# Splitting the row gathers of a graph-attention kernel into five turns behind VectorE's phases

## The reference

```
h     = max(layernorm(x), 0)
xl    = h @ hetero_w[node_type] + hetero_b[node_type]
eae   = lrelu(edge_attr @ edge_attr_w);  ete = lrelu(edge_type_emb[edge_type])
alpha = lrelu(concat(xl[dst], xl[src], ete, eae) @ att_w)
alpha = softmax of alpha over the edges that share a dst
msg   = concat(xl[src], eae) @ lin_w * alpha
out   = x + segment_sum(msg, dst)
```

## Time and profile before

| | |
|---|---|
| median of 3 runs | 5781.72 us (5751.97 to 5784.94) |
| profiled execution | 5821.55 us, its span 5819.7 us |
| PE busy | 3413.9 us, 59% of the span |
| POOL busy | 2783.2 us, 48% |
| DVE busy | 2540.0 us, 44% |
| ACT busy | 878.1 us, 15% |
| mean granted TensorE clock | 0.762 |
| DMA moved | 284.25 MB, mean 49 GB/s |

### The profile page before, as it was taken

How to read it: one execution, slowest core, us unless ns; L and a number is a source line. 1 busy time by engine, 2 the same in 40 slices (tenths; PEclk the granted TensorE clock), 3 DMA queues, 4 the chain that set the end, 5 groups by cost and what they waited for, 6 DMA issues and landing times.

```text
span 5819.7 us, 64841 instructions
## 1 busy us (share of the span) xinstructions
PE 3413.9 (59%) x21563; PEld 1921.9 (33%) x21563; DVE 2540.0 (44%) x6672; ACT 878.1 (15%) x2080; POOL 2783.2 (48%) x2793
## 2 busy tenths in 40 slices
PE   3456565665665565555666565666665666665660
PEld 2233333333333333333333333333333333333340
DVE  6343443443443444344444444444444444443464
ACT  2011111111111111111111111111111111111120
POOL 2554454454454444444554445455454454444417
PEclk7677777777787787777777777787777777777785
DMA  6111121121121121111211211211211211211112
GB/s 187 26 44 42 42 54 43 42 53 42 42 53 42 42 50 44 42 42 42 54 42 46 48 42 43 51 44 42 53 42 42 53 42 42 53 42 42 47 36 72
DMA packets 187871, 284.25 MB, mean 49 GB/s; under 512 B 74956, under 2 KB 142782, under 8 KB 186752
## 3 DMA queue, kind: packets, MB, share of 16 engines
q1 hardware_dynamic: 72864, 159.20, 9.5%
q0 software_dynamic: 90368, 55.56, 7.7%
q10 hardware_dynamic: 24288, 64.79, 3.1%
HBM read 207.03 MB, written 72.29 MB: 48 GB/s over the span
## 4 chain that ended last, share of the span: by engine, by line
another core or an unknown queue 37%; PE 29%; issue 17%; DVE 15%; POOL 2%; DMA 1%; DVEq 0%; SPq 0%; ACT 0%; POOLq 0%; ACTq 0%
PE ps_misc L678 21%; PE ps_pick L690 6%; DVE dst_f L1021 3%; DVE dscore L1055 2%; DVE sums L1148 2%; DVE gath L1048 1%; DVE node_buf L1083 1%; DVE h L1042 1%; POOL hib L515 1%; DVE onehot L1068 1%; PE ps_msg L722 1%; PE ps_attr L699 0%; DVE node_buf L1102 0%; PE ps_misc L645 0%
## 5 line engine op out<-in xcount | busy, mean ns | idle before, releaser
L481 POOL DMA_INDIRECT gath<-table_dram,meta x2675 | 2672.8, 999 | 2877.0 <-DMA meta<-meta_in 2003.3
L678 PE MATMUL ps_misc<-parts,dst_f 128*128 128x462 bf16 x9450 | 2345.3, 405 | 694.4 <-issue 615.4
L678 PEld LDWEIGHTS ps_misc<-parts,dst_f 128*128 128x128 bf16 x9450 | 988.7, 107 | 1921.5 <-issue 1187.0
L690 PE MATMUL ps_pick<-s_dst,onehot 122*128 122x128 bf16 x9375 | 736.5, 232 | 1402.7 <-DVE dscore L1055 895.8
L1055 DVE TENSOR_REDUCE dscore<-ps_pick 128x4 f32<-128x512 f32 x875 | 538.0, 629 | 1660.9 <-remote 1462.5
L690 PEld LDWEIGHTS ps_pick<-s_dst,onehot 122*128 122x128 bf16 x9375 | 609.2, 104 | 1559.0 <-DVE dscore L1055 948.5
L1042 DVE TENSOR_TENSOR h<-ps_misc,sel_mask 128x462 f32<-128x462 f32 x450 | 285.7, 635 | 1384.2 <-remote 1020.6
L575 ACT ACTIVATE wts<-args 128x50 f32<-128x50 f32 x125 | 30.7, 246 | 3484.4 <-DVE args L1126 2719.8
L588 ACT COPY rows<-sums 128x825 f32<-128x825 f32 x125 | 223.5, 1788 | 1080.6 <-DVE sums L1148 1080.6
L1021 DVE TENSOR_SCALAR dst_f<-dst_f,part_group 128x128 bf16<-128x128 f16 x1750 | 355.7, 284 | 0.9 <-DMA dst_f<-sel_code_dram 0.9
L1048 DVE TENSOR_REDUCE gath<-h 128x33 f32<-128x462 f32 x450 | 281.3, 625 | 2.7
(11 more groups left out here) (230 smaller groups left out, 1215.1 us busy)
## 6 DMA issues: line engine op xcount, KB each, us to landing
hib<-digit_dram SPq DMA_DIRECT2D x125, 612.5 KB
rows_dram<-rows ACTq DMA_DIRECT2D x125, 437.5 KB
gath<-table_dram,meta POOLq DMA_INDIRECT x2675
attr<-edge_attr_t_in SPq DMA_DIRECT2D x125, 200.0 KB
dst_f<-sel_code_dram SPq DMA_DIRECT2D x125, 128.0 KB
hib<-digit_dram SPq DMA_DIRECT2D x250, 50.0 KB
rows_dram<-gath ACTq DMA_DIRECT2D x1, 8575.0 KB, 46.8
hib<-digit_dram SPq DMA_DIRECT2D x250, 25.0 KB
```

The source lines that it names most:

```text
L481: nc.gpsimd.indirect_dma_start(gath[u][:, t, :], None, table_dram, bass.IndirectOffsetOnAxis(ap=meta_sb[u][:, t:t + 1], axis=0)).then_inc( ...
L678: last = nc.tensor.matmul(ps_sel[:, j % 2, 0:VW * GN], sel_onehot[:, g, j * P:(j + 1) * P], parts[:, k, g, :], start=(g == 0 and k == 0), ...
L690: last = nc.tensor.matmul(ps_pick[:, g % 2, j * LO:(j + 1) * LO], onehot[0:KD, t * P:(t + 1) * P], s_dst[0:KD, k, :], start=(k == 0), stop ...
```

## The change

POOL no longer issues the gathers of a chunk in one go. They are cut into five turns: tiles 0 to 4, 5 to 9, 10 to 14, 15 to 19, and the last one or two. For the gathers of chunk c each turn waits for a phase of DVE in chunk c - 2 (AHEAD = 2): the second, the fourth and the seventh of its `picks`, its `msg_added`, its `sums_ready`. Chunks 0 and 1, which have no chunk two before them, are gathered without such waits. The number of gathers, their tiles and their buffers are the same. `gather_turns` is a counter that nothing waits for.

```diff
+TURN = T // 5
+AHEAD = 2
...
-            with pool.Fori(0, ITERS) as i:
-                for u in range(U):
-                    pool.wait_ge(meta_in[u], (i + 1) * 16)
-                    pool.sem_inc(gather_turns, 1)
-                    for t in range(T - TS[u]):
+            def gather_chunk(i, u, first):
+                c = i * U + u - AHEAD
+                phases = ((picked, count(c * PICKS + 2)), (picked, count(c * PICKS + 4)), (picked, count(c * PICKS + 7)),
+                          (msg_added, count(c + 1)), (sums_ready, count(c + 1)))
+                pool.wait_ge(meta_in[u], (i + 1) * 16)
+                pool.sem_inc(gather_turns, 1)
+                for k, (phase, reached) in enumerate(phases):
+                    if not first:
+                        pool.wait_ge(phase, reached)
+                        pool.sem_inc(gather_turns, 1)
+                    for t in range(k * TURN, min((k + 1) * TURN, T - TS[u])):
                         nc.gpsimd.indirect_dma_start(
                             gath[u][:, t, :], None, table_dram,
                             bass.IndirectOffsetOnAxis(ap=meta_sb[u][:, t:t + 1], axis=0)).then_inc(gathered[u], 16)
+
+            for u in range(U):
+                gather_chunk(0, u, u < AHEAD)
+            with pool.Fori(1, ITERS) as i:
+                for u in range(U):
+                    gather_chunk(i, u, False)
```

## The result

| | before | after |
|---|---|---|
| median, in turn on one chip | 5783.33 us (5751.97 to 5799.22, 4 runs) | 4981.35 us (4966.34 to 4997.28, 4 runs) |
| profiled execution | 5821.55 us | 4997.28 us |

The account below looks back on a forecast made before the run. No busy engine but PE's matmul allowance, spent beside POOL's gathers and regained in quiet, was the bound. Start 222 + 122 x 46.1 + 2 x 19.9 + 167.7 + 1.9 = 6056, scaled by 0.9932 to 6015, said as 6010 us; range 5250 to 6450.

Parts of the forecast that it names:

- Its price: Cost of one more POOL rest a chunk: 3.3 us delay, less 1.3 us for allowance lost less, so T = 46.1 us.
- The delay: Time after a gather burst until PE's allowance returns: 3.3 us for each POOL rest, between 0.9 and 7.5.
- The usable quiet: Quiet per chunk that PE can use for matmuls: 13.3 us before, at least 10.8.
- The allowance: PE beside gathers gets through about 95 matmuls, or 70 after short quiet, then crawls; quiet gives it back.
- Number of gathers: POOL's gathers stay 2675 at 999 ns each, 27.5 us a chunk; nothing gained.
- New instructions on POOL: Five waits and five counter steps a chunk instead of one: taken as 0, upper end 146 us.
- Where the turns fall: Turns held by DVE's phases in the loop: one more POOL rest a chunk, 0.5 to 1.5 in its range.
- The start: Fewer unwaited gathers in the set-up: chunk 0 ends near 222 us instead of 284, 62 us less.
- The end: POOL works two chunks ahead, so two fewer chunks run in silence: 52 us more; last stage stays 167.7 us.
- one more rest at a delay of 7.5 us: Alternative case of the slower-still rival in the loop, said to give the same 6414 us; rival's chance 15 in 100.
- The faster rival: Short turns never spend PE's allowance, so no crawl: T 39.9 us, 5263 us; 27 in 100.
- The rival "no change": Turns 1 to 4 run together, or PE's crawl isn't tied to gathers: T stays 44.07, 5768 us; 15 in 100.

Follow-up runs that it names:

- e8b: Kernel before, one memset (about 1 us pause) after every fifth gather: 4454.21 and 4551.02 us, ratios 0.777 and 0.794; as e8, without the hold-up, 1.0602.
- e4: Kernel before with the gathers of the first five chunks only, later chunks reusing their rows: 3388.76 us, ratio 0.5817.
- p2: Kernel before without 14 large selecting matmuls a chunk: 4096.17 us, beside 4096.68 us for the kernel before.
- e3: Kernel before, POOL waiting after every fifth gather until the chunk's gathers so far have landed: 5128.58 us, ratio 0.8804.
- e7: Kernel before, POOL filling a spare tile four times after every fifth gather, without waiting for landings: 4978.98 us, ratio 0.8691.
- e5: Kernel before, POOL waiting for landings after the 7th and 14th gather only: 4660.7 us, ratio 0.8143; without the hold-up 4575.45 us, 1.1189.
- e6: Kernel before, POOL waiting for landings once a chunk, after the 11th gather: 4880.88 us, ratio 0.852.

## Why the prediction was wrong

**The step that failed is "Its price"**, and both of its terms. It charged "3.3 us, between 0.9 and 7.5 by the three rows" for one further rest of POOL, so 6.6 us of delay a chunk, and took off 1.3 us because "rests spread out lose less allowance".

- *The delay.* Read behind runs of 20 gathers and longer, it was charged behind runs of five. It is real behind long ones, 2.9 us in the mean behind 20 to 22 gathers. Behind at most 12 it is 0.4 us. The sum of a chunk is 2.3 us, 4.3 less than forecast and less than the 3.2 of before: more rests, but a smaller total.
- *The usable quiet.* POOL is quiet for 1104.1 us in 122 chunks, 9.1 us in each; without the delays 6.8 are left, where the forecast had 13.3 - 1.3 = 12.0 and called 10.8 the least that is possible. That is 5.2 us less. With the delay set right alone, T would have been 46.1 - 4.3 = 41.8 and the forecast some 5490 us: faster, but by 5% and not by 14%.

The two together are 9.5 us; the gathers' own 1.1 us more goes against them, and 46.1 - 9.5 + 1.1 = 37.7, measured 37.5. The text called the delay behind a short turn its weakest point; it gave the rival built on it 27 in 100. All three rows behind 3.3 came from long bursts, and so were no evidence on short ones.

**The allowance** failed too. It was taken as 95 matmuls, or 70 behind 10.6 us of quiet, which PE spends beside gathers and gets back in silence. The changed kernel's long run had 184 behind a pause of 2.87 us. And the sentence that DVE "waits for PE" hid that most of the products waited for were done. Both the missing delay behind short runs and the late signals would fit a backlog that grows during a run of gathers and is worked off behind it: a short run leaves little to work off. That reading is argued, not shown; no row shows such a backlog itself. Some of the gathers in the long run took 1.67 and 2.07 us instead of 0.95, beside long instructions of DVE, and e8b shows that 1.01 us between two gathers does much; a stretched gather may act as such a gap. No run tested that.

The other steps:

- *Number of gathers*: 2675, as forecast, but 1052 ns each instead of 999, 1.1 us more a chunk. Without the hold-up they take 1118. DVE's busy share in the three is 44, 51 and 62%, and the gathers that are longer lie beside its long instructions, as the two at 2260.15 and 2262.12 do.
- *New instructions on POOL*: nothing, as taken. A turn whose phase is past costs 0.31 us between gathers instead of 0.30 (the row at 2245.02).
- *Where the turns fall*: 1.6 waits a chunk, so 0.6 more rests, within the 0.5 to 1.5 that were given.
- *The start*: chunk 0 ends at 220.2, forecast 222.
- *The end*: two chunks behind the last gather, as forecast. The last stage is unchanged: 167.8 us.
- *DVE's wait for* `gathered`: none, as forecast. The waits after have no such row.
- *The sum* with T as measured: 220 + 122 x 37.46 (218.26 to 4788.58) + 37.1 + 167.8 + 1.8 = 4997. Of the 1059 us between forecast and profiled execution, 122 x (46.1 - 37.46) = 1054 are T, and the start and the end were right.
- *A slip in a rival*: "one more rest at a delay of 7.5 us" would be 44.07 + 7.5 - 1.3 = 50.3 us a chunk, about 6520 us, and not "the same" as 6414.

**The faster rival** had the direction and the condition: no crawl and next to no delay with short turns. That the turns stay short was only partly so, 72 of the 194 runs still have 20 gathers and more. Its T of 39.9 was high because it kept 10.8 us of usable quiet as the least; its half a delay (1.65 us) was a little under the 2.3 us measured.

**The rival "no change"** rested on the mechanism that PE does not depend on the gathers. Where there is a hold-up it is wrong: the same kernel runs a chunk in 44.07 us with gathers and 23.8 without (e4), and the changed kernel's pauses make it 14% faster. Where there is no hold-up it is right to 0.3%: ratio 1.0033, and all turns run together, as it said. The Trainium skill's "PE and ACT never wait on anyone" (SBUF — State Buffer, Who interferes with whom) agrees with the jobs of 4090 us. It does not cover those of 5700 us, where PE's matmuls in the set-up start 2.8 us apart with nothing to wait for; whether a port of SBUF is what it lacks there, no run shows.

## What to carry to other kernels

A delay measured behind a long burst is not a price per burst: before it is charged to a shorter one, it needs a bound of zero, and if the sign of the forecast hangs on it, a chance near one half. Before an engine is called slow, pair its products with the instructions that read them: here most of the waiting came after the product was done. Where engines starve beside a stream of another engine's DMA issues though none is at its peak, a gap of 1 to 2 us in every five to seven of them was worth 12 to 22%. Gaps that a wait makes only when the consumer is late cost next to nothing where there is no starvation (0.3% here), forced ones do (6 to 12%). And time the kernel before again in each job: a gain that undoes a hold-up is only there when the hold-up is.

## What the runs showed of the hardware

- **Beside indirect DMAs that POOL issues back to back, DVE can see PE's products late, and PE can be held up.** DVE, which was waiting for it, read a product 21.85 us after it was done; in the runs without the hold-up such a wait ends at most 0.11 us after. In the set-up of before PE starts 24 matmuls in 66.9 us, in p2 without the hold-up 509. It ends some 3.5 us behind a run of 31 gathers. Gaps of 2.1 us or more after every fifth gather prevent it, with POOL idle (e3) or filling a tile (e7); gaps of 1.0 us halve it (e8b).
- **The hold-up goes with the job, not with the kernel or the chip's number.** In each job all runs of before agree to 1.2%: 5751.97 to 5799.22 us in the job of the result, 5807.71 to 5837.5 us on chip 15, 5695.84 to 5763.53 on chip 3, 4079.76 to 4090.62 on chip 6, 4080.22 to 4096.07 on chip 14. Chip 4 took 4096.68 (one run) in one job and 5711.55 to 5757.68 in a later one. What differs between the jobs I found in no profile.
- **No version is the fastest in both conditions.** With the hold-up e8b (0.777 to 0.794), e5 (0.8143), e6 (0.852) and the changed kernel (0.8619) are in this order; without it before is best, the changed kernel 0.3% behind, e8 6.0% and e5 11.9%. A wait for a phase is the only pause tried that vanishes by itself.

Still open: through what PE and its signals are held up, and what is counted until it begins.
